# One decoder layer on one core: scores from split operands in one-pass products, key matrix in two slots, centred output weights, and new orders on every engine

## What is computed

```
attn:  q, k = elu(x Wq + bq) + 1, elu(x Wk + bk) + 1;  v = x Wv + bv      (16 heads of 8)
       k = k / sqrt(sum(k*k) + 1e-6);  out = ((q k^T) v) Wo + bo           (no softmax)
       y = x + out, normalised with gamma and beta
cross: softmax((x Wq)(ctx Wk)^T / 8) (ctx Wv), 16 heads of 64, then Wo
ffn:   fp4_linear(silu(fp4_linear(x, w_gate)) * fp4_linear(x, w_up), w_down)
       fp4_linear(a, w): both rounded to a grid of 8 magnitudes, in blocks of 16
                         scaled by the largest magnitude of the block; width 352
```

## Time and profile before

| what | value |
|---|---|
| time, median of 3 runs | 372.71 us (372.67 to 373.03) |
| span of the profiled execution, first to last instruction | 371.1 us |
| the median less this span (launch and end, outside the trace) | 1.6 us |
| TensorE matmul busy | 349.7 us, 94% |
| VectorE busy | 308.7 us, 83% |
| GpSimd busy | 269.0 us, 73% |
| ScalarE busy | 253.6 us, 68% |
| mean granted TensorE clock | 0.999 of full |

### The profile page before, as it was taken

The page is one execution under the profiler, slowest core; times in us unless marked ns, Lnnn a source line. Parts: engine busy times, 40 slices in busy tenths (PEclk is TensorE's granted clock), DMA queues, the critical chain, the costliest instruction groups (busy, mean ns, idle before and its releaser), DMA issues.

```text
span 371.1 us, 7329 instructions
## 1 busy us (share of the span) xinstructions
PE 349.7 (94%) x2147; PEld 267.9 (72%) x2147; DVE 308.7 (83%) x858; ACT 253.6 (68%) x533; POOL 269.0 (73%) x453
## 2 busy tenths in 40 slices
PE   8999989999998999999999999999999999998774
PEld 7788646675775868787678877786767787887653
DVE  3998557567689998869989779979998998999994
ACT  2957766577676677678688767878767666864553
POOL 4404459958988699969689895898988569784535
PEclk9999999999999999999999999999999999999999
DMA  8900100001000001000000000100000000000010
GB/s 248 305 2 16 30 1 16 14 16 29 15 17 14 17 0 44 28 18 16 29 14 17 14 1 17 31 0 0 17 15 2 15 2 1 15 16 14 3 30 28
DMA packets 13586, 10.44 MB, mean 28 GB/s; under 512 B 971, under 2 KB 12396, under 8 KB 13548
## 3 DMA queue, kind: packets, MB, share of 16 engines
q1 hardware_dynamic: 12540, 7.89, 7.1%
q10 hardware_dynamic: 1008, 2.10, 1.7%
HBM read 7.88 MB, written 2.10 MB: 27 GB/s over the span
## 4 chain that ended last, share of the span: by engine, by line
PE 70%; DVE 9%; POOL 8%; issue 6%; ACT 4%; DMA 1%; SPq 0%; POOLq 0%; DVEq 0%
PE A L2892 13%; PE S L2862 12%; PE TP L2852 7%; PE F L2916 6%; PE TP L2880 6%; PE A L2936 5%; PE S L2871 3%; PE A L2813 2%; PE TP L2791 2%; POOL pe L440 2%; PE F L2791 2%; PE S L2791 2%; PE TP L2925 2%; PE A L2826 2%; PE A L2821 1%
## 5 line engine op out<-in xcount | busy, mean ns | idle before, releaser
L440 POOL TENSOR_TENSOR pe<-pe,srec 128x1024 f32<-128x1024 f32 x32 | 60.9, 1904 | 9.2 <-DVE srec L1860 8.9
L2862 PE MATMUL S<-M,x1T 128*128 128x512 f32 x128 | 60.7, 597 | 1.5 <-ACT pe L1076 1.4
L2892 PEld LDWEIGHTS A<-wvoT,wqkT 128*128 128x128 f32 x480 | 56.4, 192 | 3.1 <-issue 1.8
L2892 PE MATMUL A<-wvoT,wqkT 128*128 128x128 f32 x480 | 58.0, 276 | 0.1
L434 POOL TENSOR_TENSOR fold<-pe 128x512 f32<-128x512 f32 x32 | 40.9, 1277 | 14.6 <-ACT pe L1076 14.4
L1843 DVE TENSOR_REDUCE smax<-S 128x16 fp32r<-128x1024 f32 x32 | 38.7, 1211 | 3.3 <-PE S L2862 3.1
L1076 ACT ACTIVATE pe<-S 128x1024 f32<-128x1024 f32 x32 | 32.6, 1019 | 10.6 <-PE S L2871 10.3
L1081 ACT ACTIVATE wqkT<-TP 128x1024 f32<-128x1024 f32 x32 | 32.6, 1018 | 4.3 <-PE TP L2880 4.1
L2862 PEld LDWEIGHTS S<-M,x1T 128*128 128x128 f32 x128 | 22.2, 190 | 18.3 <-issue 15.3
L2916 PE MATMUL F<-w_gu_r,GT 128*128 128x352 f32 x168 | 35.1, 344 | 0.1
L2880 PE MATMUL TP<-ident,pe 128*128 128x128 f32 x256 | 33.5, 274 | 1.6 <-POOL pe L440 0.9
(11 more groups left out here) (247 smaller groups left out, 888.2 us busy)
## 6 DMA issues: line engine op xcount, KB each, us to landing
xT<-in_x_t SPq DMA_DIRECT2D x16, 128.0 KB, 2.2
x_sb<-in_x SPq DMA_DIRECT2D x16, 128.0 KB, 2.2
out<-yf SPq DMA_DIRECT2D x15, 128.0 KB, 1.8
M<-in_fw SPq DMA_DIRECT2D x1, 560.0 KB, 11.0
wqkT<-in_wq_t ACTq DMA_DIRECT2D x2, 256.0 KB, 4.6
wqkT<-in_wk_t ACTq DMA_DIRECT2D x2, 256.0 KB, 6.1
ctx_f<-in_ctx_t ACTq DMA_DIRECT2D x2, 256.0 KB, 7.0
wvoT<-in_wv_t ACTq DMA_DIRECT2D x1, 512.0 KB, 9.4
```

The lines of the kernel that those rows point to most:

```text
L440: ge.tensor_tensor(w, w, spread(srec[n % NFO][:, :], HX, R), ALU.mult).then_inc(pn_made, 1)
L2862: last = te.matmul(S[:, half * BANK:half * BANK + BANK], x1T[b % 2][:, t * P:t * P + P], M[:, b // BH, HC * half:HC * half + HC, b % BH * ...
L2892: last = te.matmul(part(A2, t), pT[n % 2][:, j, :], vo[b % 2][:, j, :], start=(j == 0 and b not in SUM_ON_PE), stop=(j == NJ - 1))
```

## The change

- **Scores.** x1^T and M are held as fp32r high and low parts. `scores` is six fp32r products of 512 columns for a tile, in place of four fp32 instructions. `keep_x1T` (ACT) writes the high part, a new `keep_x1T_low` (DVE) the low one out of S, and `scores` waits for it.
- **M in two slots.** M is made for 4 batches at a time (`GB = 4`, 256 columns), two heads to a bank, in 4 groups of 8 steps, each of six products. `MR` has two slots of a group. Each step is kept by ACT (`m_keep_high`) and then DVE (`m_keep_low`). Groups 0 and 1 go to the banks F, TP and S; groups 2 and 3 all go to A1 and stand between `scores(3, 1)` and `scores(10, 0)`. Ahead of the first `scores` stand 13 of the 32 steps.
- **No masks.** The integer ANDs are gone: ACT writes fp32r from the source, DVE (for the context GpSimd) subtracts that from the source. So `context_cut`, `g_cut_high`, `gate_up_cut`, `gate_up_high`, `xf_cut_high` are gone; the low parts of the gate weights move from GpSimd to DVE.
- **Zero row mean.** The rows of `wo` and of the down weights are centred (DVE and GpSimd at the start: `wo_sums`, `wo_means`, `wo_centred`; a product with `centre` in place of the transpose). The norms after cross attention and feed-forward have no mean any more: ACT makes sums of squares (`squares`, 64 in all), GpSimd `square_eps` and `rstd_of`, ACT a scaled copy. `statistics`, `aggregate`, `minus_mean`, `shift_of` of these two norms are gone.
- **Roots in pairs.** The Newton iteration runs once for two batches, on 64 numbers.
- **Orders.** All five lists are new. SP now loads `fw` first and x^T of batch 0 as its eighth. Batch 15's `gate_up` is fp32r as well.

```diff
-        M = sb("M", [P, 2, HX, BH * R])
+        MR = sb("MR", [P, 2, 2, HX, GB * R], FP32R)
...
+        M_BANKS = ((F0, F1, TP0, TP1, S0, S1, F0, F1), (TP0, TP1, S0, S1, F0, F1, TP0, TP1), (A1,) * 8, (A1,) * 8)
...
-            load_xT(0)
+            sp.dma_start(fw, fw_in).then_inc(fw_loaded, 16)
             sp.dma_start(w_attn[:, :], attn_w).then_inc(aw_loaded, 16)
+            sp.dma_start(wvoT[:, 1, :, :], wo_in.rearrange("(j p) n -> p j n", p=P)).then_inc(o_loaded, 16)
             sp.dma_start(kv_bias, attn_rows[0:2 * P].partition_broadcast(NBR)).then_inc(aw_loaded, 16)
             load_xT(1)
+            load_xT(2)
+            sp.dma_start(rows[:, 2 * P:5 * P], attn_rows[2 * P:5 * P].partition_broadcast(P)).then_inc(rows_loaded, 16)
+            load_xT(0)
...
+            def square_eps(n, b):
+                pool.wait_ge(sq_made[n], T * b + T)
+                wait_free(pool, rstd_made[n], b)
+                ge.tensor_scalar(veps[n][:, :], sq[n][b % 2][:, :], 1.0 / D, LN_EPS, ALU.mult, ALU.add).then_inc(veps_made[n], 1)
...
+            def m_keep_high(g, j):
+                act.wait_ge(m_made, NJ * g + j + 1)
+                sc.activation(m_slot(g, j, 0), by_head(m_bank(g, j)[:, :], 2), ACT.Copy).then_inc(m_high, 1)
...
+                sc.activation(x2[b % 3][:, NBX * t:NBX * t + NBX, 0:BLK], blocks(y[b % 2][:, t, :], NBX), ACT.Square,
+                              accum_out=sq[n][b % 2][:, t:t + 1]).then_inc(sq_made[n], 1)
...
+            def m_keep_low(g, j):
+                dve.wait_ge(m_high, NJ * g + j + 1)
+                ve.tensor_tensor(m_slot(g, j, 1), by_head(m_bank(g, j)[:, :], 2), m_slot(g, j, 0).bitcast(FP32),
+                                 ALU.subtract).then_inc(m_low, 1)
+
+            def keep_x1T_low(b):
+                dve.wait_ge(x1T_kept, b + 1)
+                ve.tensor_tensor(x1T[b % 2][:, 1, :], S[:, 0:T * P], x1T[b % 2][:, 0, :].bitcast(FP32),
+                                 ALU.subtract).then_inc(x1T_low, 1)
...
-                    last = te.matmul(S[:, half * BANK:half * BANK + BANK], x1T[b % 2][:, t * P:t * P + P],
-                                     M[:, b // BH, HC * half:HC * half + HC, b % BH * R:b % BH * R + R],
-                                     start=True, stop=True)
+                    for n, (left, right) in enumerate(PARTS):
+                        last = te.matmul(S[:, half * BANK:half * BANK + BANK], x1T[b % 2][:, left, t * P:t * P + P],
+                                         MR[:, b // GB % 2, right, HC * half:HC * half + HC, b % GB * R:b % GB * R + R],
+                                         start=(n == 0), stop=(n == len(PARTS) - 1), skip_group_check=True)
```

More of the change, by code:

```diff
@@ new lines, in _ @@
+            keep_xfT(0)
+            keep_pT(1, 1)
+            softmax_exp(2, 1)
+            context_high(1)
+            post_norm(3, 0)
+            post_norm(3, 1)
+            squares("cross", 1, 0)
+            gate_tanh(0, 0)
+            q_negative(4)
+            q_exp(4)
+            squares("cross", 1, 1)
+            k_squares(6)
+            keep_x1T(3)
+            keep_vo(3)
+            cross_norm(1, 0)
+            cross_norm(1, 1)
+            k_exp(7)
+            keep_v(7)
@@ new lines, in _ @@
+            keep_pT(4, 1)
+            squares("ffn", 1, 0)
+            squares("ffn", 1, 1)
+            keep_x1T(6)
+            h_magnitudes(2)
+            squares("cross", 4, 0)
+            ffn_norm(0, 0)
+            keep_kvo(7)
+            squares("cross", 4, 1)
+            keep_vo(6)
+            keep_xfT(3)
+            m_keep_high(2, 6)
+            gate_tanh(3, 0)
+            softmax_exp(5, 1)
+            q_negative(8)
+            ffn_norm(0, 1)
+            keep_hT(2)
+            q_exp(8)
@@ L1395, in _ @@
+            keep_pT(5, 0)
+            k_exp(10)
+            squares("ffn", 2, 0)
+            keep_v(10)
             keep_kvo(8)
             post_norm(7, 0)
+            keep_pT(5, 1)
+            x2_magnitudes(4)
+            ffn_norm(1, 0)
             post_norm(7, 1)
+            k_squares(10)
+            softmax_exp(6, 1)
+            squares("ffn", 2, 1)
+            h_magnitudes(3)
+            keep_x1T(7)
+            squares("cross", 5, 0)
+            keep_xfT(4)
+            ffn_norm(1, 1)
@@ L1635, in _ @@
             h_magnitudes(11)
+            squares("ffn", 10, 0)
+            keep_xfT(12)
+            squares("ffn", 10, 1)
+            squares("cross", 13, 0)
+            squares("cross", 13, 1)
             keep_pT(14, 1)
@@ new lines, in _ @@
+            squares("ffn", 11, 1)
+            squares("cross", 14, 0)
+            squares("cross", 14, 1)
+            keep_xfT(13)
+            softmax_exp(15, 1)
+            cross_norm(14, 0)
+            cross_norm(14, 1)
+            h_magnitudes(12)
+            gate_tanh(13, 0)
+            x2_magnitudes(14)
+            keep_vo(15)
+            keep_xfT(14)
+            keep_pT(15, 0)
+            gate_tanh(13, 1)
+            gate_tanh(14, 0)
+            ffn_norm(10, 1)
+            keep_hT(12)
@@ new lines, in _ @@
+            attn_residual(2)
+            k_features(4)
+            aggregate("post", 1)
+            statistics("attn", 2)
+            m_keep_low(1, 5)
+            aggregate("attn", 2)
+            m_keep_low(1, 6)
+            m_keep_low(1, 7)
+            score_max(0, 1)
+            score_sums(0, 0)
+            hw_keep(1)
+            score_reciprocals(0, 0)
+            statistics("post", 2)
+            keep_x1T_low(1)
+            score_sums(0, 1)
+            aggregate("post", 2)
+            keep_kvT(3)
```

3515 lines of the change are left out of this document (1579 added, 1936 removed).

## The result

The changed kernel takes 366.37 us (median of 4 runs, 365.79 to 367.74) against 372.87 us of the kernel before on the same chip: a ratio of 0.983, with an interval of 0.981 to 0.985. That is 6.5 us less where 10.7 were forecast; it lies in the range and in case (A). The profiled execution of the changed kernel has a span of 366.0 us and is the slowest of its four (367.74), so its own difference in span is 5.1 us.

A forecast was written before the change was run, and what follows sets the result against it. TensorE's matrix work plus its idle time was taken as the bound. From a span of 371.1 us, -11.2 + 1.1 + 8.9 - 4 - 5.5 gave 360.4, or 362.0 as median; range 353 to 372.

The forecast's parts named there:

- case (A): Whole kernel: matrix gain real, the start gives most away, gaps and tail decide; 357 to 367 us, chance 0.42.
- Scores and key matrix: TensorE: a tile of scores 1.37 us for 1.72, 11.2 us less in all; key matrix 1.1 us more.
- Case (C): TensorE: products not as short as the chain says, because of weight loads; 370 us, chance 0.12.
- upper bound of 0.160: Key matrix: a product of 256 columns costs at most 0.160 us, as 352 columns do; 8.9 us more.
- Late start: Start: loads for bias rows and x^T of batch 0 come late, first m_product at 20.7 us; 8.9 us lost.
- case (B): Start: not late, as fw loads faster or its early quantising spares VectorE later work; 353 us, chance 0.22.
- VectorE's total: VectorE over the whole kernel: 24 us less busy time, some 285 us; pays only in gaps.
- Gaps in the middle: TensorE from 50 to 120 us: steps of M serve as filler, 4 of 5 us regained; bounds 0 and 5.
- Tail: From 328 us on: VectorE's dropped statistics, aggregates and masks, less two low parts, save 5.5 us; bounds 0 and 8.
- The sum: Profiled span 371.1 us: -11.2 + 1.1 + 8.9 - 4 - 5.5 = 360.4, median 362.0.
- (D): Bank A1, middle: 16 steps of M there make TensorE wait 1.3 us each; 383 us, chance 0.13.
- (E): Scores wait for the low part of x1^T on VectorE, 8 us exposed; 370 us, chance 0.11.

The follow-up runs named there:

- e5: Changed kernel with scores in fp32 products as before, on the high parts alone (low parts made but not read): 376.65 us.
- e3: Changed kernel with the warming loop repeated 45 times in place of 13, filling TensorE's idle time at the start: 366.35 us.
- e8: Kernel before with the changed kernel's first ten loads on SP, no engine's order touched: 380.85 us, ratio 1.021.
- e1: Changed kernel with x^T of batch 0, attention weights and bias rows first in SP's loads again, no engine's order touched: 367.07 us.
- e2: As e1, with fw's quantising moved behind G's low parts on VectorE and its magnitudes behind the high parts on ScalarE: 366.47 us.
- e10: As e2, with context_low(0) and k_norm(0) ahead of x_plus_rows(0) on GpSimd and x(0) loaded earlier: 366.44 us.
- e11: e10 with SP's middle order of e6 (x(9) loaded behind x(8)): 366.1 us.
- e14: As e11, with all steps of the feed-forward weights, transposes included, behind the first scores, wo_centred behind x_plus_rows(0), fw loaded last: 365.92 us.
- e13: e11 with the weights' quantising and magnitudes behind the first two key batches' features, and wo_centred behind x_plus_rows(0): 369.49 us.
- e6: Changed kernel with load_x(9) moved behind load_x(8) in SP's list: 365.86 us.

## Why the prediction was right, and where its terms were off

**Scores and key matrix.** Both terms were right: 1.39 us a tile for 1.37, 0.120 us a product for 0.120. e5 shows the scores' price at the end, 10.3 us of the 11.2. Case (C), loads that aren't hidden, is out, and so is the upper bound of 0.160. The Trainium skill ("TensorE: Matmul & The Clock Gate", LDWEIGHTS) gives a load of 128 columns some 107 ns: each of the 192 products has one, and the chain has 0.120 us for both together, so the loads run beside the products here too. The trace records a mean of 0.189 us for each of these loads, more than the page's figure, and still a product and its load take 0.120 on the chain:

```profile
L2647 PEld LDWEIGHTS A<-ctx_r,GT 128*128 128x128 f32 x96 | 13.1, 189 | 1.0 <-DVE MR L1685 0.4
```

**Late start.** The mechanism and its size were right as idle time: 6.5 us more idle up to 20.7, and about 2.5 at the lower clock, make 9.0 for 8.9. Bias rows, x^T(0) and the first `m_product` came within 1 us of the forecast. The clock at the lower level was named and priced as hidden, and e3 shows that. The further claim, that in time for the loads this term would be 0 and case (B) gives 353 us, is wrong for this kernel. e8 shows that the kernel before pays 8.0 us for such loads. But in the changed kernel the repairs of e1, e2, e10, e11 and e14 gained between -0.7 and +0.5 us, with medians that all lie within the changed kernel's own range (365.79 to 367.74), and that of e13 lost 3.1. The prediction looked for one wait where there is a row of them in five queues, and behind them, up to 60 us, the first groups' work on VectorE and GpSimd. Whether a better order of all lists would bring the start's 8 us to the end stays open: e14 brought them to batch 0 and lost them by batch 2.

**The ramp.** From 20.7 to 50 us the forecast had no term, since TensorE was busy for all of these 29.3 us before. It misses 2.8 now, in three waits of 1.05, 0.38 and 1.39 us, all for VectorE. The first and the last:

```profile
32.64 0.70 PE L2679 MATMUL A<-xT,w_attn 128*128 128x256 f32 x2 [1.05 <-DVE fk L1746]
...
41.66 1.16 PE L2626 MATMUL TP<-wvoT 64*128 64x128 f32 x16 [1.39 <-DVE MR L1685]
```

VectorE has 15 low parts of M there where it had 12 copies of M, two low parts of G, and the statistics of five norms in place of three; of the passes over `fw` three fall there, and four did before. It is busy for 27.6 of 29.3 us (22.5 before). This is the first step that failed: VectorE "pays only in gaps" was said, but not where its new work falls.

**VectorE's total.** Forecast were 24 us less and some 285; the page has 14.0 less and 294.7. The sum was made from the durations of groups, and by these it is right: all of VectorE's groups add up to 355.6 us before and 333.2 after, 22.4 less. But instructions that follow one another overlap, the short ones (statistics, aggregates, roots) most for their length, so that the busy time fell by less. ScalarE is the same case: 279 us were forecast, 25 more than before; its groups add up to 23.2 more (279.1 to 302.3), and its busy time grew by 9.8 to 263.4.

**Gaps in the middle.** 4 us were taken; from 50 to 320 TensorE's idle time fell by 3.5 (7.2 to 3.7), nearly all of it before 120. Of the 1.4 us left between 80 and 120, 1.2 are the wait behind the long issue on SP's queue, which e1, e2, e3 and e10 don't have. In e1 TensorE is idle for 0.7 us from 50 to 120, for 5.2 before, so that 4.5 came for the 4 forecast.

**Tail.** Here 5.5 us were taken as VectorE's whole relief. TensorE's idle time behind 320 us fell by 11.9 - 9.3 = 2.6. From the last `probabilities` to the end the kernel before takes 36.4 us and the changed kernel 28.9, which is 7.5 less, but that instruction itself starts 2.4 us later (GpSimd's timelines):

```profile
334.70 1.90 POOL L440 TENSOR_TENSOR pe<-pe,srec 128x1024 f32<-128x1024 f32 x1 [1.35 <-DVE srec L1860]
```
```profile
337.08 1.91 POOL L449 TENSOR_TENSOR pe<-pe,srec 128x1024 f32<-128x1024 f32 x1 [1.51 <-DVE srec L1815]
```

So the 7.5 us are counted from a point that the new orders delay. The last softmax exponential starts 2.8 us earlier than before (327.91 us for 330.66), and from it to the last `probabilities` it is 9.2 us in place of 4.0: `fold_halves` now stands behind `x_dequantise` on GpSimd and starts 3.8 us after the exponential has ended (0.2 before), and on VectorE three steps of the gate stand between `score_sums` and `score_reciprocals` where one did. From the last exponential to the end the gain is 2.3 us (40.4 to 38.1). The step of this term that failed is that the relief was taken whole, without asking what the new lists put into the last batch's softmax.

**The sum.** 10.7 us were forecast. Less the ramp (2.8), the tail (5.5 - 2.6 = 2.9) and the middle (4 - 3.5 = 0.5) they are 4.5; matrix work and start together, forecast as 1.2 less, came out as 8.3 - 6.5 = 1.8 less, which adds 0.6. That is 5.1, the measured change of the span. The terms are the rows of the table put in the forecast's words, so they have to add up; the causes stand in the paragraphs above. The median moved by 6.5, as the profiled execution is the slowest of the four.

**Rivals.** (D) did not come: ScalarE waited 4.5 us in all for the products into A1, as the group below says, and no group of TensorE's stood over 1.4 us for VectorE's copies of them. (E) did not come either; scores waited 1.2 us for the low part.

```profile
L905 ACT ACTIVATE MR<-A 128x512 fp32r<-128x512 f32 x16 | 9.5, 594 | 4.5 <-PE A L2647 4.5
...
L2721 PE MATMUL S<-MR,x1T 128*128 128x512 f32 x192 | 52.8, 410 | 1.2 <-DVE x1T L1690 1.2
```

## What to carry to other kernels

A wait at the head of an in-order queue hides the next one: before a repair is priced, follow the order of every engine past the wait, and look when each lead is gone, batch by batch, not only at the end. A profile in which one engine is busy for 93% doesn't say that the second one is free: with VectorE at 81%, 14.7 us more of it cost 8.0, while 14.7 us less matrix work gave 4.0, although the place of the added work may be part of the 8.0. A gain that one profiled execution shows is to be looked for in other kernels with the same lists, before it is put down to an edit: here e6's 1.2 us were in e1 and e10 too. Add busy times of engines from the page's first part, not from the durations of groups, when many small instructions fall away.

## What the runs showed of the hardware

The granted clock fell after 7.4 us without matrix work: 0.63 in the mean from 6.7 to 20.7 us, with `g_product` at 2.08 us and then, at 20.5 us, at 1.16. The same work can get another clock: from 325 to 330 us TensorE was busy for 3.05 us in e10 and for 3.18 in e6, and from 330 to 335 the granted clock was 0.66 in e10 and 1.00 in e6.

VectorE's pass over 1120 columns takes 1.3 us alone (and 1.31 in e10) but 2.27 in the changed kernel, where GpSimd works on `x_plus_rows(0)` and the context at the same time, 2.68 in e14 beside `probabilities`, and 3.04 in e13 beside `wo_centred`; GpSimd's `context_low(0)` took 2.37 us beside it and 1.26 alone:

```profile
16.57 2.37 POOL L413 TENSOR_TENSOR ctx_r<-ctx_f,ctx_r 128x512 fp32r<-128x512 f32 x1
```
```profile
21.73 3.04 DVE L1725 SCALAR_TENSOR_TENSOR ffn<-ffn 128x1120 f32<-128x1120 f32 x1
```

A square with a sum on ScalarE is two instructions in the trace, 0.30 and 0.19 us. The forecast took 0.49 for both:

```profile
L981 ACT ACTIVATE x<-yx 128x128 f32<-128x128 f32 x32 | 9.6, 300 | 1.3 <-DVE yx L1820 0.8
...
L981 ACT ACTIVATION_READ_ACCUMULATOR x<-yx 128x1 f32 x32 | 6.1, 189 | 0.0
```
